# Recommendation tower on one core: half of the last chunk's first dense layer put ahead of the last sums, and its relus shared between two engines

## The chip, the core and the metric

The kernel runs on one core of one Trainium2 chip. The metric is the device time of one execution in microseconds (us), from the launch to the end. Five engines work side by side, each through its own queue in program order: TensorE (PE, with its weight loads shown apart as PEld), VectorE (DVE), ScalarE (ACT), GpSimd (POOL) and SyncE (SP), which here only issues transfers. They wait for one another by semaphores.

## The reference

1024 rows have 32 fields each. For every row, each field's id picks a vector of 64 numbers from that field's table. For each of the 496 pairs of fields, z is a bilinear form of the two vectors with a 64x64 matrix of the pair. z and 16 dense numbers (512 in all) go through three dense layers:

```
p = emb_inputs[:, ROW_IDX];  q = emb_inputs[:, COL_IDX]
z = jnp.einsum('bne,hne,bnh->bn', p, kernel, q)
h = jnp.concatenate([z, dense_ctx], axis=1)
h = jnp.maximum(h @ W_top1 + b_top1, 0.0)      # 512 -> 512
h = jnp.maximum(h @ W_top2 + b_top2, 0.0)      # 512 -> 256
y = h @ W_top3                                 # 256 -> 1
```

All of it is float32. In the trace one float32 matmul of the program shows as two weight loads and two MATMUL records.

## The kernel before

The 1024 rows are worked in four chunks of 256 (`CHUNKS`, `CHUNK`). GpSimd gathers the table rows of a chunk; TensorE transposes them (L457), VectorE keeps the transposed vectors in `emb` (L397).

A chunk's bilinear work is 64 units (`NU`), 256 in all (`NUNIT`). A unit is a handful of matmuls into one of three pairs of PSUM banks, `bil[0]` to `bil[2]` (L489 for "inner" and "fields" units, L474 for "batch" units), and a multiplication of the result by the partner's vectors on VectorE (L418, L425 to L429 into `prod` and `inner`; L409 into `rows_prod` for "batch" units). VectorE counts finished units in `unit_multiplied`. Products of "batch" units are summed along their rows by ScalarE (L343). Products of the other units are summed by TensorE, four units at a time: `reduce_batch(b)` multiplies them by a selector and adds them up in `z_ps` (L509). There are 12 such batches in a chunk; batch b waits for its last unit and is put three units later in TensorE's order (`REDUCE_LAG`). After batch 8 of a chunk ScalarE copies `z_ps` into the first half of `z_sb` (groups 0 and 1 of the four groups of 128 inputs, L353, `copy_z(q, 0)`). After batch 12 TensorE adds what ScalarE summed (`turn`, L523), and ScalarE copies the second half (`copy_z(q, 1)`, groups 2 and 3); both count `z_copied`.

A chunk's dense layers are four pieces (`PIECES`): l1a and l1b are the first layer, two of its four blocks of 128 outputs each (16 matmuls together, L533), l2 the second layer (8 matmuls, L538), l3 the third (4 small matmuls, L543). After each piece ScalarE applies bias and relu, 128x256 at a time (L361, L365), or copies y (L368), and counts `head_kept`. `head_done` counts TensorE's pieces. The pieces of chunks 0 to 2 are put between units of the next chunk (`HEAD_AT`) and use the bank `side_ps`. The last chunk's pieces come after everything else, one after the other, in the first banks of `bil[0]`, `bil[1]`, `bil[2]`, `bil[0]`.

So the end of TensorE's order is: units 254 and 255 (L489; their pairs of banks are `bil[1]` and `bil[2]`, that of unit 253 is `bil[0]`), batch 47 (L509, the only one left after the loop; it waits for VectorE's product of unit 255), `turn` (L523), then for chunk 3 l1a, l1b (waiting for the second copy of z), l2 (waiting for all four relus) and l3 (waiting for both relus). SP waits for the last `head_kept` and stores y.

Of the kernel before, what the change touches and what calls it, by code (L numbers as in the profile page):

```python
# [9 lines left out]
ALU = mybir.AluOpType  # L10
ACT = mybir.ActivationFunctionType
AXIS = mybir.AxisListType

P = 128
BATCH, FIELDS, EMBED, DENSE = 1024, 32, 64, 16
HIDDEN1, HIDDEN2 = 512, 256
CHUNK = 256
CHUNKS = BATCH // CHUNK
CT = CHUNK // P
TILES = BATCH // P  # L20
# [3 lines left out]
MT1, MT2 = HIDDEN1 // P, HIDDEN2 // P  # L24
BANK = 512
GROUPS = 4
# [40 lines left out]
NUNIT = CHUNKS * NU  # L67
# [7 lines left out]
BIL_RING, PROD_RING, ROWS_RING, IN_RING = 3, 8, 3, 4  # L75
# [109 lines left out]
def reduce_unit(b):  # L185

    return unit_at((b + 1) * BATCH_UNITS - 1) + REDUCE_LAG
# [6 lines left out]
PIECES = ["l1a", "l1b", "l2", "l3"]  # L194
KEPT_BEFORE = [0, 2, 4, 6]
KEPT = 7
HEAD_AT = {reduce_unit((q + 1) * BATCHES + i + 1): (q, i) for q in range(CHUNKS - 1) for i in range(len(PIECES))}


# [3 lines left out]
BANKS_OF = {use: at % BIL_RING for at, use in enumerate(USES)}  # L203
# [3 lines left out]
def interaction_tower(nc, ids, tables, dense_rows, k_blocks, w1, b1, w2, b2, w3, ident, selector, y):  # L207
    ctx = ExitStack()
    with ctx:
# [6 lines left out]
        def sem(name):  # L216
            return ctx.enter_context(nc.semaphore(name))
# [4 lines left out]
        b1_sb = sb("b1_sb", [P, MT1])  # L222
        b2_sb = sb("b2_sb", [P, MT2])
        w1_sb = sb("w1_sb", [P, GROUPS, HIDDEN1])
        w2_sb = sb("w2_sb", [P, MT1, HIDDEN2])
        w3_sb = sb("w3_sb", [P, MT2])
# [7 lines left out]
        z_sb = sb("z_sb", [P, GROUPS, CHUNK])  # L234
        h1_sb = sb("h1_sb", [P, MT1, CHUNK])
        h2_sb = sb("h2_sb", [P, MT2, CHUNK])
        y_sb = sb("y_sb", [P, TILES])

        bil = [pb(f"bil{i}", [P, 2, BANK]) for i in range(BIL_RING)]
        z_ps = pb("z_ps", [P, BANK])  # L240
        side_ps = pb("side_ps", [P, BANK])
# [16 lines left out]
        z_copied = sem("z_copied")  # L258
        head_done = sem("head_done")
        head_kept = sem("head_kept")  # L260
        y_stored = sem("y_stored")

        block = ctx.enter_context(nc.Block())

# [5 lines left out]
        @block.sync  # L270
        def _(sp):
            sp.dma_start(ids_sb[:, :, :], ids.rearrange("(p t) f -> p t f", p=P)).then_inc(ids_loaded, 16)

            def load_k(k):
                for first in range(2 * k * k, 2 * (k + 1) * (k + 1), K_DMA):
                    last = min(first + K_DMA, 2 * (k + 1) * (k + 1))
                    for s in range(2):
                        sp.dma_start(k_sb[s * EMBED:(s + 1) * EMBED, first:last, :].rearrange("p n h -> p (n h)"),
                                     k_blocks[:, (s * 2 * NPART + first) * P:(s * 2 * NPART + last) * P])\
                          .then_inc(k_loaded[k], 16)  # L280

            def place_dense(n):

                q, k = divmod(n, QUADS)
                if n < IN_RING:
                    sp.wait_ge(inner_cleared, 1)
                else:
                    sp.wait_ge(batch_reduced, inner_batch(n - IN_RING) + 1)
                for s in range(2):
                    sp.dma_start(inner[s * EMBED:s * EMBED + 1, n % IN_RING, 1, :],  # L290
                                 dense_rows[dense_of(k, s):dense_of(k, s) + 1, q * CHUNK:(q + 1) * CHUNK])\
                      .then_inc(dense_placed[n % IN_RING], 16)

            load_k(0)
            sp.dma_start(ident_sb[:, :], ident).then_inc(consts_loaded, 16)
            sp.dma_start(sel_sb[:, :], selector).then_inc(consts_loaded, 16)
            for n in range(IN_RING):
                place_dense(n)
            for k in range(1, 4):
                load_k(k)  # L300
            for k in range(4, QUADS):
                sp.wait_ge(emb_kept, k - 3)
                load_k(k)
            sp.dma_start(w1_sb[:, :, :], w1.rearrange("(g p) n -> p g n", p=P)).then_inc(head_loaded, 16)
            sp.dma_start(w2_sb[:, :, :], w2.rearrange("(g p) n -> p g n", p=P)).then_inc(head_loaded, 16)
            sp.dma_start(w3_sb[:, :], w3).then_inc(head_loaded, 16)
            sp.dma_start(b1_sb[:, :], b1).then_inc(head_loaded, 16)
            sp.dma_start(b2_sb[:, :], b2).then_inc(head_loaded, 16)
            for n in range(IN_RING, NQUAD):
                place_dense(n)  # L310
            sp.wait_ge(head_kept, CHUNKS * KEPT)
            sp.dma_start(y.rearrange("(p t) o -> p (t o)", p=P), y_sb[:, :]).then_inc(y_stored, 16)
            sp.wait_ge(y_stored, 16)

# [15 lines left out]
        @block.scalar  # L330
        def _(act):
            def sum_rows(u):
                q, (_, part, t) = u // NU, UNITS[u % NU]
                v = batched_before(u)
                act.wait_ge(unit_multiplied, u + 1)
                if v == 0:
                    act.wait_ge(rows_cleared, 1)
                elif v % NB == 0:
                    act.wait_ge(turned, q)
                half, col = batch_place(part)  # L340
                for x in range(16):
                    row = rows_prod[:, v % ROWS_RING, x, :]
                    last = act.activation(row, row, ACT.Copy, accum_out=z_rows[:, t, half, col + x:col + x + 1])  # L343
                last.then_inc(rows_summed, 1)

            def copy_z(q, bank):
                if bank == 0:
                    act.wait_ge(batch_reduced, q * BATCHES + GROUP_BATCHES)
                    if q:
                        act.wait_ge(head_done, (q - 1) * len(PIECES) + 2)  # L350
                else:
                    act.wait_ge(turned, q + 1)
                act.activation(z_sb[:, 2 * bank:2 * bank + 2, :].rearrange("p g b -> p (g b)"), z_ps[:, :],  # L353
                               ACT.Copy).then_inc(z_copied, 1)

            def keep_head(q, i, bank):
                act.wait_ge(head_done, q * len(PIECES) + i + 1)
                if PIECES[i] in ("l1a", "l1b"):
                    for j in range(2):
                        n = 2 * i + j  # L360
                        act.activation(h1_sb[:, n, :], bank[:, j * CHUNK:(j + 1) * CHUNK], ACT.Relu,  # L361
                                       bias=b1_sb[:, n:n + 1]).then_inc(head_kept, 1)
                elif PIECES[i] == "l2":
                    for n in range(MT2):
                        act.activation(h2_sb[:, n, :], bank[:, n * CHUNK:(n + 1) * CHUNK], ACT.Relu,  # L365
                                       bias=b2_sb[:, n:n + 1]).then_inc(head_kept, 1)
                else:
                    act.activation(y_sb[:, q * CT:(q + 1) * CT], bank[:, 0:CT], ACT.Copy).then_inc(head_kept, 1)  # L368

            for u in range(NUNIT):  # L370
                if u >= SUM_LAG and UNITS[(u - SUM_LAG) % NU][0] == "batch":
                    sum_rows(u - SUM_LAG)
                if u in REDUCED_AT:
                    q, b = divmod(REDUCED_AT[u], BATCHES)
                    if b in (GROUP_BATCHES - 1, BATCHES - 1):
                        copy_z(q, b // GROUP_BATCHES)
                if u == min(HEAD_AT):
                    act.wait_ge(head_loaded, 16 * 5)
                if u in HEAD_AT:
                    keep_head(*HEAD_AT[u], side_ps)  # L380
            for u in range(NUNIT - SUM_LAG, NUNIT):
                if UNITS[u % NU][0] == "batch":
                    sum_rows(u)
            copy_z(CHUNKS - 1, 1)
            for i in range(len(PIECES)):
                keep_head(CHUNKS - 1, i, bil[i % BIL_RING][:, 0, :])

        @block.vector
        def _(dve):
# [44 lines left out]
            for u in range(NUNIT):  # L434
                for n in TRANSPOSED_AT[u]:
                    keep_quad(n)
                multiply(u)

        @block.tensor
        def _(pe):  # L440
# [116 lines left out]
            for u in range(NUNIT):  # L557
# [4 lines left out]
                    reduce_batch(REDUCED_AT[u])  # L562
                if u in HEAD_AT:
                    side_head(u)
            last = CHUNKS - 1
            for b in range(BATCHES * CHUNKS):
                if reduce_unit(b) >= NUNIT:
                    reduce_batch(b)
            pe.wait_ge(unit_multiplied, NUNIT)
            for i in range(len(PIECES)):  # L570

                pe.wait_ge(head_kept, last * KEPT + KEPT_BEFORE[0 if PIECES[i] == "l1b" else i])
                head(last, i, bil[i % BIL_RING][:, 0, :])


# [52 lines left out]
```

## Time and profile before

| what | us |
|---|---|
| median of three runs | 472.85 (470.19 to 473.06) |
| the profiled execution | 470.26 |
| its span in the trace, first to last instruction | 468.4 |
| TensorE busy in the span | 405.4 (87%) |
| VectorE busy | 326.0 (70%) |
| ScalarE busy | 265.6 (57%) |
| GpSimd busy | 241.9 (52%) |

Times in the rows are microseconds from the start of the span; mean times of one instruction are nanoseconds. An engine's idle time stands in brackets with what ended it, as far as semaphore events tell. The ends of matmuls are modelled, so a start is safer to read than an end. The profiled execution lies 2.6 us under the median of the three runs.

### The profile page before, as it was taken

What the parts mean: (1) busy time and instruction counts of PE and PEld (TensorE: products, weight loads), DVE (VectorE), ACT (ScalarE), POOL (GpSimd) and SP (SyncE); (2) the same over time, 40 slices, a digit from 0 to 9 for tenths busy, and PEclk for the clock granted to TensorE, in tenths of its full rate; (3) what the DMA queues carried; (4) which work ended last, traced back from release to release, by engine and by line L of the source; (5) the groups of instructions that cost most, each with busy time, mean ns of one, the idle gap of its engine ahead of it and who ended that gap; (6) DMA issues with size and microseconds to landing.
All of it is one profiled execution on the core that took longest, in us unless ns stands there. A gap on an engine that the chain in (4) does not pass through costs nothing.

```text
span 468.4 us, 9503 instructions
## 1 busy us (share of the span) xinstructions
PE 405.4 (87%) x3168; PEld 241.4 (52%) x3168; DVE 326.0 (70%) x354; ACT 265.6 (57%) x2085; POOL 241.9 (52%) x260
## 2 busy tenths in 40 slices
PE   0224899999979999999979999999979999999976
PEld 0113445455545556555545556555545656555555
DVE  1113588899977565799977565799977565799920
ACT  1000486659835655659835654659835654659841
POOL 5777777777777777777777777774000000000000
PEclk9999799999999999999999999999999999999999
DMA  5777871111111111111111111110000000000000
GB/s 127 166 167 165 191 209 27 29 28 25 30 27 29 28 27 29 27 27 30 26 29 29 26 29 28 26 29 18 2 1 2 2 1 1 1 1 3 1 1 0
DMA packets 13633, 19.28 MB, mean 41 GB/s; under 512 B 5584, under 2 KB 6928, under 8 KB 13584
## 3 DMA queue, kind: packets, MB, share of 16 engines
q1 hardware_dynamic: 5392, 10.27, 9.3%
q0 software_dynamic: 8192, 8.40, 9.0%
q8 instruction: 25, 0.41, 0.4%
q14 instruction: 24, 0.20, 0.1%
HBM read 18.65 MB, written 0.00 MB: 40 GB/s over the span
## 4 chain that ended last, share of the span: by engine, by line
PE 71%; DVE 11%; issue 9%; POOL 6%; DMA 2%; ACT 1%; DVEq 0%
PE bil L489 31%; PE z_ps L509 19%; PE bil L474 10%; POOL gathered L325 6%; PE side_ps L533 5%; DVE prod L418 4%; PE side_ps L538 2%; DVE prod L425 2%; DVE rows_prod L409 2%; PE bil L533 2%; DMA gathered<-in_tbl,ids_sb 1%; DVE inner L427 1%; DVE inner L429 1%; PE bil L538 1%; PE z_ps L523 1%
## 5 line engine op out<-in xcount | busy, mean ns | idle before, releaser
L343 ACT ACTIVATE rows_prod<-rows_prod 128x64 f32<-128x64 f32 x1024 | 245.1, 241 | 130.6 <-DVE rows_prod L409 130.4
L325 POOL DMA_INDIRECT gathered<-in_tbl,ids_sb x256 | 241.7, 944 | 80.4 <-issue 77.7
L418 DVE TENSOR_TENSOR prod<-bil,emb 128x1024 f32<-128x1024 f32 x160 | 190.2, 1216 | 58.0 <-PE bil L489 58.0
L489 PE MATMUL bil<-emb,k_sb 64*128 64x256 f32 x1536 | 201.1, 396 | 15.5 <-DVE emb L397 8.5
L343 ACT ACTIVATION_READ_ACCUMULATOR rows_prod<-rows_prod 128x1 f32 x1024 | 191.7, 187 | 0.0
L489 PEld LDWEIGHTS bil<-emb,k_sb 64*128 64x128 f32 x1536 | 143.7, 191 | 92.5 <-DVE prod L418 30.1
L509 PE MATMUL z_ps<-prod,sel_sb 128*32 128x512 f32 x704 | 92.3, 598 | 1.6 <-DVE prod L418 1.6
L409 DVE TENSOR_TENSOR rows_prod<-bil,gathered 128x1024 f32<-128x1024 f32 x64 | 77.6, 1213 | 22.8 <-PE bil L474 22.8
L474 PE MATMUL bil<-k_sb,emb 64*128 64x512 f32 x256 | 69.8, 623 | 3.3 <-DVE prod L418 3.3
L457 PE MATMUL bil<-ident_sb,gathered 64*128 64x64 f32 x256 | 14.8, 238 | 37.9 <-DMA gathered<-in_tbl,ids_sb 36.2
L509 PEld LDWEIGHTS z_ps<-prod,sel_sb 128*32 128x32 f32 x704 | 19.9, 109 | 48.3 <-issue 44.3
L397 DVE COPY emb<-bil 128x512 f32<-128x512 f32 x32 | 21.8, 680 | 32.0 <-PE bil L457 31.7
L457 PEld LDWEIGHTS bil<-ident_sb,gathered 64*128 64x128 f32 x256 | 13.0, 147 | 48.7 <-issue 27.4
L474 PEld LDWEIGHTS bil<-k_sb,emb 64*128 64x128 f32 x256 | 22.3, 188 | 14.9 <-DVE prod L418 7.8
L509 PE MATMUL z_ps<-inner,sel_sb 128*32 128x512 f32 x64 | 28.5, 602 | 0.0
L425 DVE TENSOR_TENSOR prod<-bil,emb 128x512 f32<-128x512 f32 x32 | 21.8, 683 | 8.2 <-PE bil L489 8.2
L533 PE MATMUL side_ps<-z_sb,w_sb 128*128 128x256 f32 x96 | 22.3, 386 | 0.0
L533 PEld LDWEIGHTS side_ps<-z_sb,w_sb 128*128 128x128 f32 x96 | 17.8, 190 | 7.2 <-issue 5.0
L353 ACT ACTIVATE z_sb<-z_ps 128x512 f32<-128x512 f32 x8 | 4.8, 597 | 28.0 <-PE z_ps L523 26.9
L361 ACT ACTIVATE h_sb<-side_ps,b_sb 128x256 f32<-128x256 f32 x12 | 5.0, 470 | 22.7 <-PE side_ps L533 22.7
L427 DVE TENSOR_TENSOR inner<-bil,emb 64x256 f32<-64x256 f32 x32 | 13.7, 427 | 0.4
L429 DVE TENSOR_TENSOR inner<-bil,emb 64x256 f32<-64x256 f32 x32 | 13.3, 416 | 0.4
(25 smaller groups left out, 69.2 us busy)
## 6 DMA issues: line engine op xcount, KB each, us to landing
k_sb<-in_k_blocks SPq DMA_DIRECT2D x24, 256.0 KB, 4.9
gathered<-in_tbl,ids_sb POOLq DMA_INDIRECT x256, 2.5
k_sb<-in_k_blocks SPq DMA_DIRECT2D x8, 192.0 KB, 5.7
inner<-in_dense_rows SPq DMA_DIRECT2D x64, 1.0 KB
w_sb<-in_w SPq DMA_DIRECT2D x1, 1024.0 KB
k_sb<-in_k_blocks SPq DMA_DIRECT2D x8, 64.0 KB, 3.7
w_sb<-in_w SPq DMA_DIRECT2D x1, 512.0 KB
ids_sb<-in_ids SPq DMA_DIRECT2D x1, 128.0 KB, 2.1
```

The source lines that it names most:

```text
L325: pool.indirect_dma_start(gathered[:, q % 2, t, field * EMBED:(field + 1) * EMBED], None, tables[field], bass.IndirectOffsetOnAxis(ap=ids_ ...
L343: last = act.activation(row, row, ACT.Copy, accum_out=z_rows[:, t, half, col + x:col + x + 1])
L397: dve.tensor_copy(out, banks).then_inc(emb_kept, 1)
L409: dve.tensor_tensor(rows_prod[:, v % ROWS_RING, :, :].rearrange("p (j x) h -> p j (x h)", j=2), x_y[:, :, :], row.to_broadcast([P, 2, BANK ...
L418: dve.tensor_tensor(out, x_y[:, :, :], both.to_broadcast([P, 2, BANK]), ALU.mult)\
L425: dve.tensor_tensor(out[:, 0, :].rearrange("p (j b) -> p j b", j=2), x_y[:, :, 0:CHUNK], e[:, a:a + 1, :].to_broadcast([P, 2, CHUNK]), ALU ...
L427: dve.tensor_tensor(inner[EMBED:P, n % IN_RING, 0, :], x_y[EMBED:P, 0, CHUNK:BANK], e[EMBED:P, b, :], ALU.mult)
L457: last = pe.transpose(bil[BANKS_OF["quad", n]][:, s, at:at + EMBED], gathered[rows, q % 2, t, (2 * k + c) * P:(2 * k + c + 1) * P], ident_ ...
L474: last = pe.matmul(out[:, s, :], e[rows, m, t * P:(t + 1) * P], k_sb[rows, 2 * part:2 * part + 4, :].rearrange("p n h -> p (n h)"), start= ...
L489: last = pe.matmul(out[:, s, i * CHUNK:(i + 1) * CHUNK], k_sb[rows, n, :], e[rows, j, :], start=True, stop=True)
L509: last = pe.matmul(z_ps[32 * col:32 * (col + 1), :], sel_sb[:, 30 - r:62 - r], moving, start=r == 0, stop=bank == 0 and r == 30, tile_posi ...
L533: last = pe.matmul(bank[:, j * CHUNK:(j + 1) * CHUNK], w1_sb[:, g, n * P:(n + 1) * P], z_sb[:, g, :], start=g == 0, stop=g == GROUPS - 1)
```

## The change

The last chunk's dense layers are written out anew at the end of TensorE's program; everything before the end of the unit loop stays as it is, and so do the head pieces of chunks 0 to 2.

- Seven banks are named: `last_banks[0]` is `side_ps`, 1 and 2 are the two banks of `bil[0]` (unit 253), 3 and 4 those of `bil[1]` (unit 254), 5 and 6 those of `bil[2]` (unit 255). Each of the four blocks n of the first layer has its own bank (0 to 3), each block of the second (4, 5), and the third layer has bank 6.
- Right after the loop, ahead of batch 47, TensorE issues the matmuls of groups 0 and 1 for all four blocks (8 of the 16 of the first layer). It waits for the first copy of z, for chunk 2's last copy of y and, block by block, for the unit whose bank is taken.
- Batch 47 and `turn` follow; then groups 2 and 3 for all blocks, each block counted in `head_done` by itself.
- ScalarE applies the relu of blocks 0 and 2 and of the second layer's block 0; VectorE, after its product of unit 255, those of blocks 1 and 3 and of the second layer's block 1, with a `tensor_scalar` (add the bias, maximum with 0), counted in the new `vector_kept`.
- The second layer's matmuls run over the input blocks g in the outer loop and the two output blocks inside, and wait only for the relu of block g. The third layer waits for both relus.
- SP's wait counts 4 instead of 7 for the last chunk (`LAST_KEPT`).

The core of the diff (declarations left out):

```
@@ scalar
-            for i in range(len(PIECES)):
-                keep_head(CHUNKS - 1, i, bil[i % BIL_RING][:, 0, :])
+            done = (CHUNKS - 1) * len(PIECES)
+            for n in (0, 2):
+                act.wait_ge(head_done, done + n + 1)
+                act.activation(h1_sb[:, n, :], last_banks[n][:, 0:CHUNK], ACT.Relu, bias=b1_sb[:, n:n + 1])\
+                   .then_inc(head_kept, 1)
+            act.wait_ge(head_done, done + MT1 + 1)
+            act.activation(h2_sb[:, 0, :], last_banks[MT1][:, 0:CHUNK], ACT.Relu, bias=b2_sb[:, 0:1]).then_inc(head_kept, 1)
+            act.wait_ge(head_done, done + MT1 + MT2 + 1)
+            act.activation(y_sb[:, (CHUNKS - 1) * CT:TILES], last_banks[MT1 + MT2][:, 0:CT], ACT.Copy).then_inc(head_kept, 1)
@@ vector
+            done = (CHUNKS - 1) * len(PIECES)
+            for n in (1, 3):
+                dve.wait_ge(head_done, done + n + 1)
+                dve.tensor_scalar(h1_sb[:, n, :], last_banks[n][:, 0:CHUNK], b1_sb[:, n:n + 1], 0.0, ALU.add, ALU.max)\
+                   .then_inc(vector_kept, 1)
+            dve.wait_ge(head_done, done + MT1 + 2)
+            dve.tensor_scalar(h2_sb[:, 1, :], last_banks[MT1 + 1][:, 0:CHUNK], b2_sb[:, 1:2], 0.0, ALU.add, ALU.max)\
+               .then_inc(vector_kept, 1)
@@ tensor
+            q = CHUNKS - 1
+            def first_layer(n, g):
+                return pe.matmul(last_banks[n][:, 0:CHUNK], w1_sb[:, g, n * P:(n + 1) * P], z_sb[:, g, :],
+                                 start=g == 0, stop=g == GROUPS - 1)
+            pe.wait_ge(z_copied, 2 * q + 1)
+            pe.wait_ge(head_kept, q * KEPT)
+            for n in range(MT1):
+                if n:
+                    pe.wait_ge(unit_multiplied, NUNIT - 2 + (n - 1) // 2)
+                for g in range(2):
+                    first_layer(n, g)
             for b in range(BATCHES * CHUNKS):
                 if reduce_unit(b) >= NUNIT:
                     reduce_batch(b)
+            pe.wait_ge(z_copied, 2 * q + 2)
+            for n in range(MT1):
+                first_layer(n, 2)
+                first_layer(n, 3).then_inc(head_done, 1)
             pe.wait_ge(unit_multiplied, NUNIT)
-            for i in range(len(PIECES)):
-                pe.wait_ge(head_kept, last * KEPT + KEPT_BEFORE[0 if PIECES[i] == "l1b" else i])
-                head(last, i, bil[i % BIL_RING][:, 0, :])
+            for g in range(MT1):
+                if g % 2 == 0:
+                    pe.wait_ge(head_kept, q * KEPT + g // 2 + 1)
+                else:
+                    pe.wait_ge(vector_kept, g // 2 + 1)
+                for n in range(MT2):
+                    second = pe.matmul(last_banks[MT1 + n][:, 0:CHUNK], w2_sb[:, g, n * P:(n + 1) * P], h1_sb[:, g, :],
+                                       start=g == 0, stop=g == MT1 - 1)
+                    if g == MT1 - 1:
+                        second.then_inc(head_done, 1)
+            pe.wait_ge(head_kept, q * KEPT + MT1 // 2 + 1)
+            pe.wait_ge(vector_kept, MT1 // 2 + 1)
+            for t in range(CT):
+                for g in range(MT2):
+                    third = pe.matmul(last_banks[MT1 + MT2][:, t:t + 1], h2_sb[:, g, t * P:(t + 1) * P], w3_sb[:, g:g + 1],
+                                      start=g == 0, stop=g == MT2 - 1)
+            third.then_inc(head_done, 1)
```

## Rows read from the trace of the kernel before

**Rows 1.** Page, part 2: busy tenths and granted clock in 40 equal slices

```profile
PE   0224899999979999999979999999979999999976
PEclk9999799999999999999999999999999999999999
```

**Rows 2.** Chain of waits, from 443 us: start, length, engine, tile, line

```profile
448.99 1.93 PE z_ps L509 x16
450.92 0.92 PE z_ps L523 x32
451.86 0.60 ACT z_sb L353
452.46 0.14 issue
452.60 7.16 PE bil L533 x32
459.78 0.85 ACT h_sb L361 x2
460.67 3.73 PE bil L538 x16
464.43 0.85 ACT h_sb L365 x2
465.32 1.07 PE bil L543 x8
```

**Rows 3.** Waits, 440 to 468.4 us: total, times, longest

```profile
PE z_ps L509 <- DVE prod L418: 1.6, 1, 1.6
PE bil L538 <- ACT h_sb L361: 0.9, 1, 0.9
PE bil L543 <- ACT h_sb L365: 0.9, 1, 0.9
PE bil L533 <- ACT z_sb L353: 0.8, 1, 0.8
```

**Rows 4.** Stretches: length, busy PE, PEld, DVE, ACT, POOL; clock; DMA

```profile
447.40:449.00 1.60, 0.01 (x2) 0.01 (x2) 1.54 (x2) 1.60 (x15) 0.00 (x0) 1.00 0.00 0
452.60:459.80 7.20, 7.14 (x32) 5.97 (x32) 0.00 (x0) 0.86 (x3) 0.00 (x0) 1.00 0.01 2
447.30:468.40 21.10, 14.81 (x106) 11.28 (x104) 1.64 (x2) 5.06 (x24) 0.00 (x0) 1.00 0.01 1
```

**Rows 5.** Timeline of the end: start, length, engine, line, operation

```profile
445.40 2.00 PE L489 MATMUL bil<-emb,k_sb 64*128 64x256 f32 x16
446.58 2.36 DVE L418 TENSOR_TENSOR prod<-bil,emb 128x1024 f32<-128x1024 f32 x2 [0.76 <-PE bil L489]
...
456.32 0.84 ACT L361 ACTIVATE h_sb<-bil,b_sb 128x256 f32<-128x256 f32 x2 [3.87 <-PE bil L533]
459.78 0.84 ACT L361 ACTIVATE h_sb<-bil,b_sb 128x256 f32<-128x256 f32 x2 [2.62 <-PE bil L533]
...
466.61 0.37 SPq L312 DMA_DIRECT2D out_y<-y_sb  x1
```

**Rows 6.** Timeline of TensorE around a head piece of chunk 2

```profile
377.20 1.93 PE L509 MATMUL z_ps<-prod,sel_sb 128*32 128x512 f32 x16
379.06 3.72 PE L533 MATMUL side_ps<-z_sb,w_sb 128*128 128x256 f32 x16
382.71 2.00 PE L489 MATMUL bil<-emb,k_sb 64*128 64x256 f32 x16
384.54 0.41 PE L457 MATMUL bil<-ident_sb,gathered 64*128 64x64 f32 x8
```

**Rows 7.** Groups by line: count, busy us, mean ns, idle before

```profile
L418 DVE TENSOR_TENSOR prod<-bil,emb 128x1024 f32<-128x1024 f32 x160 | 190.2, 1216 | 58.0 <-PE bil L489 58.0
L425 DVE TENSOR_TENSOR prod<-bil,emb 128x512 f32<-128x512 f32 x32 | 21.8, 683 | 8.2 <-PE bil L489 8.2
L427 DVE TENSOR_TENSOR inner<-bil,emb 64x256 f32<-64x256 f32 x32 | 13.7, 427 | 0.4
L361 ACT ACTIVATE h_sb<-bil,b_sb 128x256 f32<-128x256 f32 x4 | 1.7, 469 | 6.5 <-PE bil L533 6.5
```

**Rows 8.** Timeline of ScalarE: the last chunk's first copy of z

```profile
423.49 0.60 ACT L353 ACTIVATE z_sb<-z_ps 128x512 f32<-128x512 f32 x1 [0.28 <-PE z_ps L509]
```

More of the change, by code:

```diff
@@ L196 @@
 KEPT = 7
+LAST_KEPT = 4
 HEAD_AT = {reduce_unit((q + 1) * BATCHES + i + 1): (q, i) for q in range(CHUNKS - 1) for i in range(len(PIECES))}
@@ L260, in interaction_tower @@
         head_kept = sem("head_kept")
+        vector_kept = sem("vector_kept")
         y_stored = sem("y_stored")
+        last_pairs = [bil[BANKS_OF["unit", u]] for u in range(NUNIT - 3, NUNIT)]
+        last_banks = [side_ps[:, :]] + [pair[:, x, :] for pair in last_pairs for x in range(2)]
         block = ctx.enter_context(nc.Block())
@@ L310, in _ @@
                 place_dense(n)
-            sp.wait_ge(head_kept, CHUNKS * KEPT)
+            sp.wait_ge(head_kept, (CHUNKS - 1) * KEPT + LAST_KEPT)
             sp.dma_start(y.rearrange("(p t) o -> p (t o)", p=P), y_sb[:, :]).then_inc(y_stored, 16)
@@ L564, in _ @@
                     side_head(u)
-            last = CHUNKS - 1
+            q = CHUNKS - 1
[9 more added lines that the diff above has]
+                    first_layer(n, g)
             for b in range(BATCHES * CHUNKS):
```

## The prediction

> **What bounds the kernel now.** I read the page's slices first. TensorE is busy in nine tenths or more of nearly every slice from the seventh on, at the full granted clock [rows 1], so until the units end, only less TensorE work would help, and the change takes none away there. The change touches the last 21 us alone, and there I read the chain of waits in order of time. From 448.99 us it is a single line: last sums, turn, copy of z, first layer, two relus, second layer, two relus, third layer [rows 2]. Nothing runs beside it, so each microsecond saved on it ends the kernel a microsecond earlier. Behind it come only the copy of y and its store, issued at 466.61 [rows 5].
>
> Next the waits: in which holes of this line does TensorE stand idle? There are four: 1.6 us ahead of the last sums, until VectorE has multiplied unit 255; 0.8 behind the last sums, for the copy of z; 0.9 between the first and second layer, for the relus; 0.9 between the second and third [rows 3]. The change aims at three of them. In 21.10 us from 447.30 on, TensorE works 14.81 [rows 4]; the change leaves that work as it is and moves it into the holes.
>
> **Part 1: half of the first layer ahead of the last sums.** What is the price of 8 matmuls (16 records)? In the steady run of the last chunk's first layer, ScalarE's first relu behind l1a starts at 456.32 and that behind l1b at 459.78 [rows 5]: 3.46 us for 16 records. Set between work of other shapes, as chunk 2's l1b was, 16 records take from 379.06 to the next start at 382.71, 3.65 us [rows 6]. So entering and leaving cost 0.19 together.
>
> When can it start? Units 254 and 255 start at 445.40 [rows 5]; a block of 16 such records in the loop is followed by the next start after 384.54 − 382.71 = 1.83 us [rows 6], and by their modelled end TensorE is free at 447.40. I take 447.30. The waits set in front of it are met: the first copy of z ended at 424.09, 23 us earlier [rows 8]; chunk 2's dense layers are long over; blocks 1 and 2 need unit 253, which VectorE finished before it began 254 at 446.58; block 3 needs unit 254, half-way through the 2.36 us of two products, about 447.76, and TensorE comes to it only at 447.30 + 3 x 0.87 = 449.9 [rows 5]. Nothing on VectorE waits for batch 47, so its later start holds nobody up. No transfer is moved.
>
> The last sums then start at 447.30 + 3.65 = 450.95 instead of 448.99 [rows 2], 1.96 later, and VectorE's product (done at 446.58 + 2.36 = 448.94 [rows 5]) has been ready for 2 us. The sums, the turn and the copy of z keep their lengths (1.93, 0.92, 0.60 and the 0.14 behind [rows 2]). Behind the copy only 16 of 32 records remain, 3.46 less. Term 1: 3.46 − 1.96 = **1.50 us**. Note that this gains the hole less the change of shape, not the 3.46 that are moved. Bounds: a second 0.19 for the changes of shape leaves 1.31; none at all gives 1.69.
>
> A rule speaks against this part. The Trainium skill, TensorEngine Tiling (Array Packing), section Tiling Modes (Key Properties), says that a change of the tiling mode drains TensorE. The new order changes mode once more than the old one: 64-row tiles (L489), full array (L533), 32-column tiles (L509) instead of the first straight to the last. The page gives no price; by the 0.19 measured above for a way in and a way out, the sum has it in it already, and by the rule alone nothing more could be said than that the term is under 1.69.
>
> **Part 2: the hole between first and second layer.** Before, the last sum of the first layer is seen by ScalarE at 459.78, two relus follow, and the second layer's last sum is seen at 464.43 [rows 2, 5]: 4.65 us. After, the second layer begins with block 0 of h1, whose relu started while three blocks were still to come. Is each relu in time? Blocks come 0.87 apart (3.46 / 4). A relu on ScalarE takes 0.47 [rows 7]. The latest is block 3, on VectorE: its input is complete when the second layer begins, its output is wanted after three pairs of matmuls, 3 x 0.87 = 2.6 us later; it may take five times as long as ScalarE's and cost nothing. With the cover gone it would cost its own length, about half a microsecond. So TensorE runs through and the second layer costs its steady 3.46. Term 2: 4.65 − 3.46 = **1.19 us**. If refilling TensorE costs as before although it never stops, the layer takes the 3.73 of [rows 2] and the term is 0.92. That the two output blocks alternate between two banks I cost at nothing: the units' matmuls alternate banks too and run at 1.83 us for 16 records [rows 6].
>
> **Part 3: the hole between second and third layer.** Before: 464.43 to 465.32 [rows 2], 0.89, of which two relus in a row are 0.84 (the second overlaps the first) and some 0.05 passes before TensorE moves. After: ScalarE's relu of block 0 starts one matmul (0.43) earlier and, with 0.47, ends about 0.04 behind the last sum; VectorE's starts at the last sum. No row shows a `tensor_scalar`. The nearest are VectorE's products out of PSUM: 427 ns for 256 columns, 683 for 512, 1216 for 1024 [rows 7], so about 1.04 ns a column and a fixed 0.15. I take 0.42 for 256 columns, by the row that has the same number of columns; the bounds are 0.68 (if the bias operand made it as dear as 512 columns) and nothing (then ScalarE's end sets the hole at 0.09). Hole after: 0.42 + 0.05 = 0.47. Term 3: 0.89 − 0.47 = **0.42 us**, between 0.16 and 0.80.
>
> **The rest.** The third layer, the copy of y and the store keep their lengths. The added waits are met before TensorE's program comes to them, or are the ones costed. Nothing else is late at the end: there is no other work in the last 21 us that the store could come to wait for [rows 4].
>
> Sum: 1.50 + 1.19 + 0.42 = **3.1 us**, by the bounds 2.4 (1.31 + 0.92 + 0.16) to 3.7 (1.69 + 1.19 + 0.80). Against the profiled execution: 470.26 − 3.1 = 467.2, span 468.4 − 3.1 = 465.3. That execution lies 2.6 under the median of the three runs, which spread over 2.9 us, as much as the change should bring. I expect the same spread after, so I set the sum against the median: 472.85 − 3.1 = **469.7**, 0.7% less.
>
> **Rivals.**
>
> *The change of shape eats the fill.* If the drain at the extra mode change costs TensorE the hole it was to fill, term 1 is gone and 1.6 us remain: 471.2. That needs 1.5 us where a way in and a way out cost 0.19 [rows 6]. Chance 0.08. The rule on tiling modes named above, from the Trainium skill, is what it would be by.
>
> *The change doesn't do what it says.* One of the waits ahead of the first half is met late, TensorE stands there as long as it stood ahead of the sums, and any slip behind it brings the time back to 472.9. The latest wait by the rows is met 2.1 us before it is needed (447.76 against 449.9). Chance 0.07, with other causes of no gain.
>
> *Slower: the clock.* The granted clock isn't fixed: it reads 7 tenths in the fifth slice, behind slices in which TensorE was busy for 2 to 4 tenths [rows 1]. If the new order of work made the clock fall from 2.4 to 1.2 GHz at the start of the tail, the 14.81 us of TensorE work [rows 4] would take twice as long: 472.85 − 3.1 + 14.8 = 484.6. It decides against the change once more than 3.1 us of that work runs at half clock, and by over 1% from 3.1 + 4.7 = 7.8 us. Against it: through a hole of 1.6 us and three of 0.8 to 0.9 the clock stayed at 1.00 in every stretch [rows 3, 4], and the change closes holes. The Trainium skill, TensorE: Matmul & The Clock Gate, Part 1, says the throttled state is the default and activity releases it, which would make more activity the safer side too. Chance 0.03.
>
> **How the numbers follow.** The forecast has 0.82, the fill eaten 0.08, no gain 0.07, slower by the clock 0.03. About 1%, 4.7 us, is what a measurement of this kernel can tell from no change. A gain of 3.1 is inside it from 472.85; but the times shown lie in two groups, 470.2 (with the profiled one) and about 473, and if the median of the runs after falls into the lower one it is 470.2 − 3.1 = 467.1, 1.2% under 472.85. I give that a third of the forecast: 0.27 faster by over 1%. The other 0.55, and 0.15 of the first two rivals, are within 1%: 0.70. Slower by over 1%: 0.03.
>
> The range goes from the lower group with the largest sum, 470.2 − 3.7 = 466.5, to the upper group with the fill eaten, 473.1 − 1.6 = 471.5. Outside stay no gain, the clock, and some of the tails: less than 2 in 10.
>
> **What would show each step right or wrong.** Right: 16 records of the first layer between L489 and L509, starting at about 447.3; last sums at about 451.0 with no wait for VectorE; second copy of z at about 453.8; second layer following the first without a hole and its last sum about 7.2 us after the first layer's second half began; one hole of about 0.5 us ahead of the third layer, which starts at about 462.2; clock 1.00 throughout. Wrong: last sums later than 451.2 (change of shape), a wait for VectorE or ScalarE inside the second layer (relu late), a hole of 0.7 or more ahead of the third (dear `tensor_scalar`), a clock under 1.00 in the tail. The prediction as a whole is wrong if the tail shortens as worked out and the runs don't follow.

## The result and the profile after

The changed kernel's median is 469.16 us (15 runs, 466.77 to 472.56) against 471.94 for the kernel before (15 runs in turn with them, 470.09 to 475.04). The ratio is 0.9936, 95% interval 0.9913 to 0.996: faster by 0.6%, inside the 1% named ahead. Forecast were 469.7, a range of 466.5 to 471.5, and 3.1 us off; the medians lie 2.8 apart, and the ratio times 471.94 is 3.0 off.

The profiled execution of the changed kernel took 469.98 us, with a span of 468.2. That is only 0.3 and 0.2 less than the one of before, so the gain has to be looked for in the tail, and what took it back elsewhere. First the chain of waits of the changed kernel from its last units on (start, length, engine, tile, line, with pauses of 0.02 us left out; L512 the units, L592 the first layer, L532 the sums, L546 the turn, L616 the second layer, L459 VectorE's relu, L624 the third layer):

```profile
448.22 1.93 PE bil L512 x16
450.15 1.06 PE side_ps L592 x4
451.21 2.59 PE bil L592 x12
453.80 1.85 PE z_ps L532 x16
455.66 0.92 PE z_ps L546 x32
456.60 0.61 ACT z_sb L361
457.20 0.04 issue
457.25 1.13 PE side_ps L592 x4
458.38 2.59 PE bil L592 x12
460.97 3.47 PE bil L616 x16
464.46 0.50 DVE h_sb L459
464.95 0.14 issue
465.09 1.04 PE bil L624 x8
466.15 0.17 ACT y_sb L401
```

Against [rows 2], TensorE now goes from the units into the first layer and from there into the sums, and from the second half of the first layer straight into the second layer. In the timeline (start, length, engine, line, operation, idle before) the 16 records of units start at 448.15, and VectorE sees the last sum of the first layer at 461.00 and that of the second at 464.46:

```profile
448.15 2.00 PE L512 MATMUL bil<-emb,k_sb 64*128 64x256 f32 x16
...
461.00 0.48 DVE L456 TENSOR_SCALAR h_sb<-bil,b_sb 128x256 f32<-128x256 f32 x1 [1.24 <-PE bil L592]
...
464.46 0.48 DVE L459 TENSOR_SCALAR h_sb<-bil,b_sb 128x256 f32<-128x256 f32 x1 [2.97 <-PE bil L616]
```

From 448.15 to the copy of y at 466.15 it is 18.00 us. Before it was 466.41 − 445.40 = 21.01 [rows 5], with the copy of y at 466.41 in the chain. The tail is 3.0 us shorter. Of the four waits of [rows 3] two are left, both shorter (waits of TensorE from 440 us on: what waited, for what, total, times, longest):

```profile
PE side_ps L592 <- ACT z_sb L361: 0.7, 1, 0.7
PE bil L624 <- DVE h_sb L459: 0.7, 1, 0.7
```

What took 2.75 us back lies ahead of the tail (448.15 against 445.40). VectorE's copies of the transposed vectors, for which TensorE waits at the starts of chunks 1, 2 and 3, show where (chains of waits; first the kernel before, then the changed one):

```profile
135.55 0.61 DVE emb L397
240.88 0.61 DVE emb L397
346.21 0.61 DVE emb L397
...
135.00 0.61 DVE emb L412
241.97 0.61 DVE emb L412
348.96 0.61 DVE emb L412
```

The changed kernel's execution is 0.55 us ahead at the first, 1.09 behind at the second and 2.75 behind at the third, and it stays 2.75 behind up to the tail. So it lost 1.64 us between the first two and 1.66 between the next two. Here are stretches around the starts of chunks 1 and 2: from to, length, busy time of PE, PEld, DVE, ACT, POOL, then the granted clock and DMA. The changed kernel:

```profile
132.00:136.00 4.00, 1.44 (x20) 1.17 (x20) 3.56 (x6) 0.70 (x6) 3.08 (x4) 1.00 0.15 25
136.00:141.00 5.00, 5.00 (x40) 2.41 (x40) 3.26 (x5) 0.00 (x0) 3.78 (x5) 0.66 0.14 30
...
242.00:247.00 5.00, 4.38 (x32) 3.01 (x36) 3.01 (x6) 0.00 (x0) 3.78 (x5) 0.66 0.16 30
```

The kernel before:

```profile
136.00:141.00 5.00, 4.80 (x72) 3.05 (x72) 3.41 (x6) 0.00 (x0) 3.78 (x5) 1.00 0.14 30
...
242.00:247.00 5.00, 5.00 (x76) 3.10 (x74) 3.26 (x5) 0.38 (x1) 3.78 (x5) 1.00 0.15 30
```

Code and order are the same there. At the start of a chunk TensorE stands still for some 2.6 us, because the first units wait for VectorE's copy. In the changed kernel's execution the clock then fell to its lower level for a part of the stretch, after two of the three starts; in the execution of before after none. In stretches of 1 us (columns: from to, length, PE, granted clock, DMA) it reads half:

```profile
138.00:139.00 1.00, 1.00 (x8) 0.50 0.14 35
```

1.00 − 0.66 over 5 us is 1.7 us of full clock lost, each time, about what the copies show. So a comparison of the two profiled executions as wholes would have said "no gain".

### The profile page after: what moved, and what is told of

It reads as the page before. It is cut to its first block, busy times and chain, and to the rows that moved or that the text cites. A ratio compares the mean times of both kernels' runs of the same rounds, so it can differ in the third digit from the quotient of the medians.

```text
span 468.2 us, 9504 instructions
## 1 busy us (share of the span) xinstructions
PE 407.6 (87%) x3168; PEld 242.2 (52%) x3168; DVE 327.5 (70%) x357; ACT 264.5 (57%) x2082; POOL 241.9 (52%) x260
## 4 chain that ended last, share of the span: by engine, by line
PE 72%; DVE 11%; issue 8%; POOL 6%; DMA 2%; ACT 0%; DVEq 0%
PE bil L512 31%; PE z_ps L532 19%; PE bil L497 10%; POOL gathered L333 6%; PE side_ps L556 5%; DVE prod L433 4%; PE side_ps L561 2%; DVE prod L440 2%; DVE rows_prod L424 2%; DMA gathered<-in_tbl,ids_sb 1%; DVE inner L442 1%; DVE inner L444 1%; PE bil L592 1%; PE z_ps L546 1%; PE bil L616 1%
## 5 line engine op out<-in xcount | busy, mean ns | idle before, releaser
L512 PE MATMUL bil<-emb,k_sb 64*128 64x256 f32 x1536 | 202.4, 398 | 15.6 <-DVE emb L412 8.5
L512 PEld LDWEIGHTS bil<-emb,k_sb 64*128 64x128 f32 x1536 | 144.2, 191 | 92.9 <-DVE prod L433 30.2
L532 PE MATMUL z_ps<-prod,sel_sb 128*32 128x512 f32 x704 | 93.2, 604 | 0.0
L532 PEld LDWEIGHTS z_ps<-prod,sel_sb 128*32 128x32 f32 x704 | 20.1, 110 | 47.5 <-issue 45.1
L532 PE MATMUL z_ps<-inner,sel_sb 128*32 128x512 f32 x64 | 28.5, 601 | 0.0
```

The source lines that it names most:

```text
L512: last = pe.matmul(out[:, s, i * CHUNK:(i + 1) * CHUNK], k_sb[rows, n, :], e[rows, j, :], start=True, stop=True)
L532: last = pe.matmul(z_ps[32 * col:32 * (col + 1), :], sel_sb[:, 30 - r:62 - r], moving, start=r == 0, stop=bank == 0 and r == 30, tile_posi ...
```

## Experiments

All times are of the stretch from the start of the last 16 records of units to the start of the copy of y, read from the timeline, where nothing else is said: 21.01 us before, 18.00 changed. The theory was that each of the three terms is a hole closed by itself. The rivals: the change of shape eats the fill; VectorE's help, not the order of the matmuls, closes the holes behind the layers; holes don't matter, only TensorE's work does.

### The first half back behind the turn

```
-            for n in range(MT1):
-                if n:
-                    pe.wait_ge(unit_multiplied, NUNIT - 2 + (n - 1) // 2)
-                for g in range(2):
-                    first_layer(n, g)
+            pe.wait_ge(unit_multiplied, NUNIT - 1)
...
             for n in range(MT1):
-                first_layer(n, 2)
+                for g in range(3):
+                    first_layer(n, g)
                 first_layer(n, 3).then_inc(head_done, 1)
```

> The changed kernel with part 1 alone undone: all 16 matmuls of the last chunk's first layer stand behind the turn again; the shared relus and the order of the second layer stay. Measure: from the start of the last 16 records of units to the copy of y, 21.01 us in the kernel before and 18.00 in the changed one. Theory (the hole ahead of the last sums was filled): the hole of 1.6 us comes back and the stretch is 18.00 + 1.5 = 19.5. Rival (the change of shape ate the fill): it stays at 18.0 to 18.3.

Measured: 444.84 to 464.38, 19.54 us, and the hole is back (timeline of this kernel; in brackets the idle time and what ended it):

```profile
444.84 2.00 PE L512 MATMUL bil<-emb,k_sb 64*128 64x256 f32 x16
446.02 2.36 DVE L433 TENSOR_TENSOR prod<-bil,emb 128x1024 f32<-128x1024 f32 x2 [0.76 <-PE bil L512]
448.52 1.92 PE L532 MATMUL z_ps<-prod,sel_sb 128*32 128x512 f32 x16 [1.69 <-DVE prod L433]
```

Undoing part 1 costs 19.54 − 18.00 = 1.54 us. The change of shape didn't eat the fill. What the other two parts bring without it is 21.01 − 19.54 = 1.47. Some 0.1 us of the 1.54 is this kernel's own: its hole is 1.69 where it was 1.59. The same product of VectorE releases the same sums, but in this kernel another wait stands directly ahead of that for unit 255, and TensorE starts 0.14 behind VectorE's end instead of 0.04 (chains of waits; the kernel before, then this one):

```profile
448.95 0.04 issue
...
448.39 0.14 issue
```

The kernel's median, 470.51 (10 runs), has a ratio of 0.9959 [0.9925, 0.9994] to the kernel before.

### All relus on ScalarE

```
-                if g % 2 == 0:
-                    pe.wait_ge(head_kept, q * KEPT + g // 2 + 1)
-                else:
-                    pe.wait_ge(vector_kept, g // 2 + 1)
+                pe.wait_ge(head_kept, q * KEPT + g + 1)
```

(and VectorE's three relus on ScalarE, block by block in the same order)

> The changed kernel with all six relus of the last chunk on ScalarE, block by block; first half ahead and order of the second layer stay. Theory (it is the order of the second layer, with a wait for each block, that closes the holes behind the first and second layer): no hole inside or ahead of the second layer; ahead of the third layer the two relus overlap the last sum, hole 0.46 to 0.50 where VectorE's 0.48 relu leaves 0.63, so 17.85 to 17.9 us in place of 18.00. Rival (VectorE's share closes them): the hole ahead of the third layer goes back to 0.9 and TensorE waits in the second layer: 18.3 to 19.5.

Measured: 446.96 to 464.88, 17.92 us: 0.08 shorter than with VectorE's help. The end of its chain of waits:

```profile
459.77 3.04 PE bil L607 x14
462.81 0.02 issue
462.83 0.91 ACT h_sb L400 x2
463.74 0.04 issue
463.79 1.07 PE bil L614 x8
```

The first relu of the second layer starts before the last sum is there, so the two in a row end soon after it. TensorE follows the relus' end after 0.04 to 0.05 us where it followed VectorE's after 0.14; this kernel also has one wait ahead of the third layer where the changed one has two in a row. The rival falls: VectorE's help isn't what closes the holes. With the second layer running over its input blocks outside and output blocks inside, and waiting block by block, one engine is enough for the relus. The order without the waits is the next kernel; the waits with the old order, output blocks outside, were not tried.

### One wait for all four relus

```
+            pe.wait_ge(head_kept, q * KEPT + MT1 // 2)
+            pe.wait_ge(vector_kept, MT1 // 2)
             for g in range(MT1):
-                if g % 2 == 0:
...
```

> The changed kernel with one wait for all four relus ahead of the second layer, as in the kernel before; the sharing with VectorE and the first half ahead stay. Theory: the last relu (0.48) and its signal (0.14) stand ahead of the layer and TensorE refills (0.3): hole of 0.6 to 0.65 and 18.00 + 0.9 = 18.9 us. Rival (sharing the relus is enough to close that hole): 18.0 to 18.2.

Measured: 447.91 to 466.81, 18.90 us, with the wait where it was expected (timeline):

```profile
460.76 0.48 DVE L456 TENSOR_SCALAR h_sb<-bil,b_sb 128x256 f32<-128x256 f32 x1 [1.24 <-PE bil L592]
461.39 3.69 PE L614 MATMUL bil<-h_sb,w_sb 128*128 128x256 f32 x16 [0.67 <-DVE h_sb L456]
```

So of the 1.19 us of part 2, 0.29 come without the waits by block, since one relu and not two is left behind the last sum; whether that takes the second engine, or only that each block is counted by itself, this kernel doesn't tell. Waiting block by block gives the other 0.90.

### Two of the eight matmuls behind the turn

```
-            for n in range(MT1):
+            for n in range(MT1 - 1):
...
+            pe.wait_ge(unit_multiplied, NUNIT - 1)
+            for g in range(2):
+                first_layer(MT1 - 1, g)
             pe.wait_ge(z_copied, 2 * q + 2)
```

> The changed kernel with the fourth block's two matmuls of the first half moved from ahead of the last sums to behind the turn, into the 0.72 us in which TensorE waits for the copy of z. Theory (a moved matmul gains only where it lies in a hole; the first hole needs 1.6 us, six matmuls are 2.6): last sums 0.87 earlier, the hole behind the turn closed, 18.00 - 0.70 = 17.3 us. Rival (the tail is bound by TensorE's work alone, holes do not matter): 18.0.

Measured: 448.02 to 465.23, 17.21 us, 0.79 less than the changed kernel, with the same TensorE work. Six matmuls still fill the first hole, and the two others now run while ScalarE copies z (timeline):

```profile
455.46 1.13 PE L592 MATMUL bil<-z_sb,w_sb 128*128 128x256 f32 x4
455.60 0.60 ACT L361 ACTIVATE z_sb<-z_ps 128x512 f32<-128x512 f32 x1 [3.91 <-PE z_ps L546]
456.43 1.03 PE L592 MATMUL side_ps<-z_sb,w_sb 128*128 128x256 f32 x4
```

The rival, that only the amount of work counts, falls. The kernel's median, 468.79 (10 runs, 467.93 to 472.12), can't tell 0.8 us from the spread of the runs.

### Work that nobody reads in the holes at the starts of chunks

The spread of the runs was as large as the gain, so its cause was worth runs of its own.

```
+            def fill(q):
+                if q > 1:
+                    pe.wait_ge(head_kept, (q - 1) * KEPT)
+                for _ in range(2):
+                    pe.matmul(side_ps[:, :], k_sb[:, 0, :], k_sb[:, 0:4, :].rearrange("p n h -> p (n h)"),
+                              start=True, stop=True)
...
                     transpose_quad(n)
+                    if n > QUADS and n % QUADS == 1:
+                        fill(n // QUADS)
```

> The changed kernel with two matmuls of 512 columns that nobody reads (1.73 us) put into the 2.55 us hole in which TensorE waits for VectorE's copy at the start of chunks 1, 2 and 3; they only add work. It tests why runs of one kernel spread from 466.8 to 472.6: in the profiled execution of the changed kernel the granted clock fell to half level behind two of these holes, in that of the kernel before behind none. Theory (the clock falls there in some runs, by the hole): no half clock after the first 60 us, mean granted clock of every run 0.992 or 0.993, times within 466.5 to 468. Rival (the spread has nothing to do with these holes): times as spread as before, 466.8 to 472.6, median 469.2 or more.

Measured: median 466.90 (6 runs, 466.60 to 467.71), every run with a mean granted clock of 0.993; ratio to before 0.9904 [0.988, 0.9927]. With added work the median lies 2.3 us under that of the changed kernel (the two were not run in turn; against the kernel before, in turn with each, it is 5.0 and 2.8 us). The spread went from 5.8 us to 1.1, with 6 runs in place of 15; the 11 runs of the kernel before in turn with these spread over 3.2. The same stretches as above, in this kernel:

```profile
132.00:136.00 4.00, 3.36 (x26) 1.85 (x22) 3.83 (x6) 0.97 (x9) 3.08 (x4) 1.00 0.12 27
136.00:141.00 5.00, 5.00 (x74) 3.09 (x76) 3.27 (x5) 0.00 (x1) 3.78 (x5) 1.00 0.15 30
...
242.00:247.00 5.00, 5.00 (x76) 3.09 (x74) 3.26 (x5) 0.60 (x1) 3.78 (x5) 1.00 0.15 26
```

The tail, 445.06 to 463.05, is that of the changed kernel (17.99). What the idle work takes away is the fall of the clock behind the hole.

### Useful work in those holes

```
+            def first_half(q):
...
+                pe.wait_ge(z_copied, 2 * q + 1)
+                pe.matmul(side_ps[:, :], zeros[:, 0:P], zeros[:, :], start=True, stop=False)
+                for n in range(2):
+                    for g in range(2):
+                        pe.matmul(side_ps[:, n * CHUNK:(n + 1) * CHUNK], w1_sb[:, g, n * P:(n + 1) * P], z_sb[:, g, :],
+                                  start=False, stop=False)
...
-                        for g in range(GROUPS):
+                        for g in range(2 if i == 0 else 0, GROUPS):
```

(called where `fill` was, for the chunk that has just ended; the second line of the diff's end is l1a)

> The changed kernel with the same move for chunks 0 to 2: in the 2.55 us hole at the start of the next chunk TensorE issues groups 0 and 1 of the first two blocks of the first layer into side_ps (4 matmuls, 1.73 us, behind one short bf16 matmul of zeros that opens the bank's sums), and l1a later issues groups 2 and 3 only. Theory (moved work gains where a hole was): three times 1.7 us less TensorE work behind the holes, less the change of shape of l1a that stays: 4 to 5 us off, and by the clock theory no half clock behind the holes, so 462 to 463.5. Rival (the work behind is bound by VectorE, not TensorE): 0 to 2 us off.

Measured: median 461.65 (6 runs, 460.88 to 462.35), ratio to before 0.9786 [0.9762, 0.981], 5.25 us under the kernel with the idle work: three times four matmuls of 0.43 are 5.2. The moved work is gained whole, a little more than the 4 to 5 expected against an undisturbed run, and the median lies just under the expected 462. The first start of a chunk (timeline of TensorE):

```profile
133.25 0.39 PE L588 MATMUL side_ps<-zeros 128*128 128x512 bf16 x1
133.47 1.89 PE L591 MATMUL side_ps<-z_sb,w_sb 128*128 128x256 f32 x8
135.87 1.14 PE L516 MATMUL bil<-emb,k_sb 64*128 64x256 f32 x8 [0.50 <-DVE emb L415]
```

### Everything together

The kernel above, two matmuls behind the turn as in the fourth experiment, and the third layer by input blocks:

```
+            for g in range(MT2):
+                if g == 0:
+                    pe.wait_ge(head_kept, q * KEPT + MT1 // 2 + 1)
+                else:
+                    pe.wait_ge(vector_kept, MT1 // 2 + 1)
+                for t in range(CT):
+                    third = pe.matmul(third_banks[t][:, 0:1], h2_sb[:, g, t * P:(t + 1) * P], w3_sb[:, g:g + 1],
+                                      start=g == 0, stop=g == MT2 - 1)
```

> The kernel above, with two matmuls of the last first half behind the turn and the third layer ordered so that its two matmuls on block 0 run while VectorE applies the relu of block 1. Theory: 0.7 less for the first, 0.4 to 0.5 for the second, 1.1 to 1.2 below the kernel above: stretch from the last units to the copy of y 16.8 to 16.9 us, time 461 to 462.5. Rival (one of the two is hidden by something else): 17.3 or 17.5.

Measured: 438.85 to 455.56, 16.71 us, 1.29 less than the kernel above (18.00) where 1.1 to 1.2 were expected; median 460.92 (6 runs, 459.43 to 461.57), ratio to before 0.9774 [0.975, 0.9799]. The medians of the two lie only 0.7 apart, less than the 2.1 over which its runs spread. It is the fastest kernel of this study, 2.3% under the one before. In the timeline the third layer now starts 0.10 behind the start of VectorE's relu:

```profile
453.94 0.47 ACT L403 ACTIVATE h_sb<-bil,b_sb 128x256 f32<-128x256 f32 x1 [3.41 <-PE bil L638]
454.37 0.48 DVE L465 TENSOR_SCALAR h_sb<-bil,b_sb 128x256 f32<-128x256 f32 x1 [2.97 <-PE bil L638]
454.47 1.05 PE L648 MATMUL bil<-w_sb,h_sb 128*128 128x1 f32 x8
455.56 0.17 ACT L405 ACTIVATE y_sb<-bil 128x2 f32<-128x2 f32 x1 [1.14 <-PE bil L648]
```

### VectorE's relu without the bias operand

```
-... last_banks[n][:, 0:CHUNK], b1_sb[:, n:n + 1], 0.0, ALU.add, ALU.max)
+... last_banks[n][:, 0:CHUNK], 0.0, 0.0, ALU.add, ALU.max)
```

> The changed kernel in which VectorE's three relus add the constant 0 in place of the bias read from memory, so three of the six bias additions of the last chunk are left out of the computation. It asks why VectorE's relu took 0.48 us where 0.42 was worked out. Theory (the bias operand costs the difference): 0.42 us a relu, hole ahead of the third layer 0.57 and the stretch from the last units to the copy of y 17.94 in place of 18.00. Rival (a relu of 256 columns out of PSUM costs that anyway): 0.48, hole 0.63, 18.00.

Measured, one execution: 0.42 us in place of 0.48, TensorE stands 0.61 us ahead of the third layer where it stood 0.67, and the stretch is 17.94, as the theory had it:

```profile
463.81 0.42 DVE L459 TENSOR_SCALAR h_sb<-bil 128x256 f32<-128x256 f32 x1 [3.03 <-PE bil L616]
464.38 1.02 PE L624 MATMUL bil<-w_sb,h_sb 128*128 128x1 f32 x8 [0.61 <-DVE h_sb L459]
```

The bias read per partition costs the 0.06.

## Why the prediction was right, step by step

The marks it gave, or that follow from its terms, as distances from the start of the last 16 records of units (445.40 before, 448.15 after):

| step | forecast | measured |
|---|---|---|
| first half begins | 1.90 | 1.93 |
| last sums begin | 5.55 | 5.58 |
| second half begins | 9.16 | 9.10 |
| last sum of the first layer seen | 12.88 | 12.85 |
| last sum of the second layer seen | 16.34 | 16.31 |
| third layer begins | 16.81 | 16.94 |
| copy of y begins | 17.90 | 18.00 |

**Term 1**, 1.50 forecast, is 1.47 by the marks: the last sums began 5.58 into the stretch where they began 448.99 − 445.40 = 3.59 [rows 2, 5], 1.99 later, and 3.46 − 1.99 = 1.47. The kernel without it gives 1.54, with 0.1 of its own. The first half took 453.80 − 450.15 = 3.65 us in the chain, as chunk 2's piece did [rows 6]: 0.19 above its steady 3.46, once. The Trainium skill, TensorEngine Tiling (Array Packing), section Tiling Modes, says that a change of mode drains TensorE; the trace agrees in so far as the way in and the way out cost 0.19 us together. That the drain is what costs it, no run here shows.

One length was taken as kept and wasn't: TensorE followed the copy of z after 0.14 us [rows 2] and does so after 0.04 now (457.20 to 457.25 in the chain above). That is 0.1 us which the sum didn't have.

**Term 2**, 1.19 forecast, is 4.65 − (464.46 − 461.00) = 1.19. The argument for it, that the relus are covered because the second layer takes up one block after the other, and not by the second engine, is what the kernels with the single wait (18.90) and with ScalarE alone (17.92) show.

**Term 3** was mis-sized: 0.42 forecast, 0.89 − (465.09 − 464.46) = 0.26 measured. Two of its parts were small: VectorE's relu was taken from a row with as many columns but no operand per partition [rows 7], 0.42 for 0.48; and from the end of the relu to TensorE 0.05 was taken from [rows 2], where it took 0.14. The engine is not the reason: before, TensorE followed VectorE's product after 0.04 and ScalarE's copy of z after 0.14. In each place with 0.14 the program has another wait directly ahead of the one that ends last, as the new third layer has; no run was made for that alone. With these sizes the terms add up to 1.47 + 0.10 + 1.19 + 0.26 = 3.02, and the stretch is 3.01 shorter. The value of term 3 lies within the bounds given (0.16 to 0.80). Nor was it seen that two relus in a row on ScalarE would have done as well, since the first needn't wait for the last sum: the prediction worked that relu out for block 0 and didn't carry it on to block 1.

**The rivals.** The fill was not eaten, and no wait took its place. The clock stayed at 1.00 in the tail. But it did fall, in the same kernel, at places that the change doesn't touch: the prediction looked at the clock in the tail and in the first 60 us, and took the two groups of times as given.

**The time.** The sum was set against the median and not against the profiled execution, and that was right: the profiled execution of before was one without any fall at the starts of chunks. That the medians agree within 0.5 us is in part luck: the median of 15 runs of the kernel before was 0.9 under that of the three shown, and from 471.94 the sum would have given 468.8. Against the profiled execution, 467.2 would have been forecast, and 4 of the 15 runs after lie within half a microsecond of that. Sorted by the mean granted clock, the runs of the changed kernel are:

| mean granted clock | runs | us |
|---|---|---|
| 0.992 to 0.993 | 4 | 466.77 to 467.49 |
| 0.988 to 0.989 | 8 | 468.51 to 469.98 |
| 0.985 | 2 | 470.18, 470.23 |
| 0.982 | 1 | 472.56 |

The 42 runs of the kernel before that went in turn with seven of the experiments' kernels sort the same way: nine at 0.993 with a median of 470.1, 24 at 0.988 and 0.989 (471.9), four at 0.986 (473.2) and five at 0.982 (475.6). Like against like, by the medians of the rows, the change takes 2.9, 2.6, 3.0 and 3.0 us.

One fall costs 1.7 us of clock; the rows lie 1 to 2.4 us apart, with what the start loses (below) mixed in. The third of the forecast's chance for more than 1% hung on which row the median would fall into; it fell into the second.

## What to carry to other kernels

At the end of a kernel, where one chain is left, list the holes of the bounding engine with what ends each, and move work of that engine that is already fed into them: what is gained is the hole less the changes of shape, not the work moved. Before a second engine is brought in to shorten a wait, see whether the order of the waiting work can cover it: with the input block outside, waits block by block gave 0.90 of the 1.19 us here, and one engine was enough. The holes in the steady part, repeated three times, were worth more (5.2 us) than those at the end (3.0). And where execution times fall into groups, compare like with like, or the stretch that was changed: two single executions differed by 0.3 us here, and the stretch by 3.0.

## What the runs showed of the hardware

TensorE's clock fell to its lower level, 1.2 of 2.4 GHz, in some executions and not in others, behind the same holes of some 2.6 us at the starts of chunks; each fall cost 1.7 us. Of the seven profiled executions with these holes open, two show no such fall (the kernel before, and that without the first half), two show one (all relus on ScalarE, no bias operand) and three show two (the changed kernel, one wait for all, two matmuls behind the turn). With 1.7 us of matmuls in these holes, read or not, the profiled executions show no fall behind them, and the six runs with idle work lie within 1.1 us, all at 0.993. The Trainium skill, TensorE: Matmul & The Clock Gate, Part 1, says that the throttled state is the default and activity releases it; the trace agrees, in that adding work alone kept the clock up. What decides in a given execution whether it falls was not tried. In every profiled execution the clock also stood at the lower level for 3.4 or 6.8 us between 44 and 55 us, in part while TensorE was idle, waiting for the gathers; that was left as it is.

VectorE's `tensor_scalar` of 128x256 out of PSUM took 0.42 us with constants and 0.48 with a bias per partition.

TensorE followed the end of the instruction that it waited for, on VectorE or ScalarE, after 0.04 us in most places (some 25 behind VectorE in the chain of the kernel before) and after 0.14 in a few. In each of those few the program has another wait directly ahead of the one that ends last. The kernel without the first half against the one before, 0.14 and 0.04 behind the same product, comes nearest to a test of that.
